# Expert output products: three fp16 products for all eight experts, instead of fp32 for two of the eight

## The reference

```
x = x + xattn(ctx, layernorm(x), Wq)       # q = x Wq, k = v = ctx Wq; causal softmax
xf = layernorm(x)
gates = softmax(xf @ gate_W); the two highest, normalised -> cw
out = xf
for e in range(8):
    h = relu(xf @ W1[e] + b1[e])           # 128 -> 256
    out = out + cw[:, e:e+1] * (h @ W2[e] + b2[e])   # 256 -> 128
x = x + out
```

## Time and profile before

| | |
|---|---|
| median of 3 runs | 142.91 us (142.78 to 143.04) |
| the profiled execution's own time | 143.2 us |
| its span, first to last instruction | 141.4 us |
| mean granted TensorE clock | 0.976 |
| PE matmul busy | 125.1 us, 88% |
| DVE busy | 104.9 us, 74% |
| ACT busy | 96.2 us, 68% |
| POOL busy | 47.3 us, 33% |

### The profile page before, as it was taken

How to read it: one execution, slowest core, us unless ns; L and a number is a source line. 1 busy time by engine, 2 the same in 40 slices (tenths; PEclk the granted TensorE clock), 3 DMA queues, 4 the chain that set the end, 5 groups by cost and what they waited for, 6 DMA issues and landing times. The chain is left out here.

```text
span 141.4 us, 3259 instructions
## 1 busy us (share of the span) xinstructions
PE 125.1 (88%) x1165; PEld 92.9 (66%) x1165; DVE 104.9 (74%) x413; ACT 96.2 (68%) x191; POOL 47.3 (33%) x53
## 2 busy tenths in 40 slices
PE   6987079789999699999998799999996999699992
PEld 2774055658786457887875468697864677467781
DVE  1529999998559799476586995885497994978573
ACT  3346354976959486796959476769685848689940
POOL 6380342703033750330127532130336603333500
PEclk9999956999999999999999999999999999999999
DMA  3999900000000000200000001000000002000002
GB/s 107 293 270 270 270 4 5 0 0 2 0 5 0 0 7 0 74 0 5 0 0 0 0 5 53 28 0 0 0 5 2 2 5 74 0 2 5 0 0 74
DMA packets 9872, 5.54 MB, mean 39 GB/s; under 512 B 472, under 2 KB 9856, under 8 KB 9856
## 3 DMA queue, kind: packets, MB, share of 16 engines
q1 hardware_dynamic: 9712, 5.27, 12.9%
q10 hardware_dynamic: 144, 0.07, 0.2%
HBM read 4.28 MB, written 1.05 MB: 38 GB/s over the span
## 5 line engine op out<-in xcount | busy, mean ns | idle before, releaser
L623 POOL TENSOR_TENSOR h_lo<-h,h_hi 128x512 f16<-128x512 f32 x24 | 27.9, 1162 | 67.7 <-ACT h L517 67.7
L517 ACT ACTIVATE h<-psH,b1T 128x512 f32<-128x512 f32 x64 | 43.5, 686 | 3.1 <-PE psH L347 1.8
L790 DVE SCALAR_TENSOR_TENSOR acc<-psY,weight_y,acc 128x128 f32<-128x128 f32 x125 | 35.1, 342 | 5.8 <-PE psY L368 5.3
L516 ACT ACTIVATE h_hi<-psH,b1T 128x512 f16<-128x512 f32 x48 | 33.0, 687 | 9.1 <-PE psH L347 9.0
L774 DVE TENSOR_TENSOR h_lo<-h,h_hi 128x512 f16<-128x512 f32 x24 | 17.3, 721 | 15.2 <-ACT h L517 15.2
L347 PE MATMUL psH<-x_lo,w_hi 128*128 128x512 f16 x62 | 23.8, 384 | 0.4
L343 PE MATMUL psH<-x_hi,w_hi 128*128 128x512 f16 x62 | 23.8, 384 | 0.0
L344 PE MATMUL psH<-x_hi,w_lo 128*128 128x512 f16 x62 | 23.8, 383 | 0.0
L368 PE MATMUL psY<-w_hi,h_hi 128*128 128x128 f16 x192 | 22.7, 219 | 0.0
L368 PE MATMUL psY<-w_lo,h_hi 128*128 128x128 f16 x192 | 22.7, 219 | 0.0
L368 PEld LDWEIGHTS psY<-w_hi,h_hi 128*128 128x128 f16 x192 | 15.4, 98 | 3.3
(11 more groups left out here) (169 smaller groups left out, 184.3 us busy)
## 6 DMA issues: line engine op xcount, KB each, us to landing
w_sb<-in_L_ffn_W_dram SPq DMA_DIRECT2D x8, 256.0 KB, 5.1
x_sb<-in_x_dram SPq DMA_DIRECT2D x1, 768.0 KB, 6.9
ctx_sb<-in_ctx_dram SPq DMA_DIRECT2D x1, 768.0 KB, 6.5
out_dram<-acc SPq DMA_DIRECT2D x3, 256.0 KB, 2.3
x_sb<-in_x_dram SPq DMA_DIRECT2D x1, 256.0 KB, 3.5
ctx_sb<-in_ctx_dram SPq DMA_DIRECT2D x1, 256.0 KB, 3.9
out_dram<-acc SPq DMA_DIRECT2D x2, 128.0 KB, 1.8
wq_sb<-in_L_xattn_Wq_dram ACTq DMA_DIRECT2D x1, 64.0 KB, 2.6
```

Of the source, the lines that this page charges most:

```text
L516: nc.scalar.activation(h_hi[:, C * (e % 2) + c, :], psH[c][:, :], ACT.Relu, bias=bias, scale=scale)
L517: nc.scalar.activation(h[:, C * (e % 2) + c, :], psH[c][:, :], ACT.Relu, bias=bias, scale=scale).then_inc(h_ready, 1)
L623: nc.gpsimd.tensor_tensor(h_lo[:, i, :], h[:, i, :], h_hi[:, i, :], ALU.subtract).then_inc(hlo0_ready, 1)
L790: last = nc.vector.scalar_tensor_tensor(out=o, in0=y, scalar=weight_y[:, t, e:e + 1], in1=o, op0=ALU.mult, op1=ALU.add)
```

## The change

Both sets become empty, so every expert of every group is split. Expert 0 changes in all four groups, expert 3 in groups 0 to 2, and expert 7 in group 3: eight expert-groups of 32.

```
--- before
+++ after
@@ -45,8 +45,8 @@
     SCALE = float(D) ** -0.5
     MASKED = 1e30
     SX, SW, SH = 16.0, 64.0, 16.0
-    FULL = (0, 3)
-    FULL_LAST = (0, 7)
+    FULL = ()
+    FULL_LAST = ()
     HB = 2 * C
     Y_FREE = 2
     WARM_UP = 9
```

## The result

The changed kernel takes 154.1 us (median of 4 runs, 152.44 to 155.15), the kernel before 142.97 us beside it (4 runs). The ratio is 1.0729 [1.0633, 1.0825]; it is taken from the executions in the fast state and so leaves out the one of 155.15 us, which was in the slow one. Slower, as forecast. The median of 154.1 us lies 0.4 us beyond the upper end of the range, that of the other three (153.97 us) 0.3 us, and the ratio times the kernel before (1.0729 x 142.97 = 153.4 us) just inside it: the result is at the edge. The profiled execution took 153.97 us, with a span of 152.2 us.

The account below looks back on a forecast made before the run. In-order ACT and DVE queues, with DVE's subtraction waiting for both halves of new h, decide, not busy PE. 1.1 + 3 x 0.95 + 2 x 1.0 + 1.3 + 1.0 = 8.25 us gives 151.2 us, range 148.5 to 153.7.

Parts of the forecast that it names:

- The direction: Whole kernel: the change makes it slower, given a chance of 0.93.
- rival A: Whole kernel: PE decides, late ACT and DVE work fits in gaps, 3.5 us faster, 139.4 us; chance 0.06.
- Prologue: Before group 0's key product: expert 0's relu ends later, delaying DVE's gate step and then ctxT; +1.1 us.
- rival C: New prologue: all of the forecast plus a clock fall during PE's idle time, +2.8 us, 154.0 us; chance 0.09.
- Boundaries: Groups 0 to 1, 1 to 2: DVE's subtraction delays gate step, ctxT and key product; +1.0 us each.
- Rival B: Boundaries and prologue: gate delay is absorbed before the key product and costs nothing; +2.1 us, 145.0 us; chance 0.09.
- Expert 3: Groups 0 to 2: ACT's extra reads delay expert 4's relu, DVE's subtraction, residual and xf transposes; +0.95 us each.
- Last boundary: Into the last group: late gate chain, with L754 held by POOL's subtraction, delays weight_cat; +1.3 us.
- The end: Last group: DVE's subtraction waits for expert 7's relu and stands ahead of the last sums; +1.0 us.
- The sum: All terms from prologue to end added: 8.25 us, giving 151.2 us; forecast's chance 0.72.

Follow-up runs that it names:

- e4: Changed kernel with DVE's subtraction for the next group's expert 0 moved behind the gate step, prologue included; 148.51 us.
- e2: Kernel before with expert 0 alone split, in all four groups; 149.4 us.
- e6: Changed kernel with five matmuls on zeros filling PE's gap ahead of each group's xf transposes; 151.26 us.
- e7: Kernel before with ACT also writing an unread h_hi for the fp32 experts, products and DVE and POOL work unchanged; 145.46 us.
- e5: e4 with the last group's expert 7 back in fp32 and DVE's sums of experts 2 and 3 ahead of subtractions for experts 3 and 4; 143.78 us.
- e8: Changed kernel with POOL's last-group subtraction for expert 2 waiting until DVE has written weight_cat; 153.17 us.
- e3: Kernel before with only expert 7 of the last group split; 144.6 us.
- e10: Kernel before with only POOL's last-group subtraction for expert 2 made to wait until weight_cat is written; 142.83 us.
- e1: Kernel before with expert 3 alone split, in groups 0 to 2; 147.79 us.
- e9: e5 with POOL's last-group wait of e8 added; 143.59 us.

## Why the prediction was right, and where it failed

- **The direction, and rival A.** Right. Each split product saves PE its 0.44 us and the kernel is 11 us slower. PE is the busiest engine and the change relieves it; the end is set by what PE waits for.
- **Prologue, +1.1.** Measured +1.10; e4 takes it away by DVE's order alone. PE's wait for ctxT is 1.05 us there, not the 1.9 us of rival C's working; its products before it run at the low clock until 27.1 us, before until 23.9.
- **Boundaries, +1.0 each from the queues.** Right as the cause: +1.05 in e2 and e6, where the clock holds; nothing with ACT's reads alone (e7); nothing with the gate step first (e4). Rival B is out by the same rows.
- **Expert 3, +0.95 each.** The mechanism is right: of what was added, ACT's two reads alone do it (e7), by way of DVE's subtraction for expert 4 (e5). The size was a little high: 0.82 to 0.87 us (1.04 in group 0). The working added 0.95 us to the start of probsT and took the rest as before. But probsT no longer waits for PE, and the next relu follows 0.47 us behind its start, not 0.59 us. The two relus together end 0.81 us later.
- **Last boundary, +1.3.** Measured +1.29, with the stall on L754 as forecast, and e8 takes the stall away.
- **The end, +1.0.** Measured +1.01, and +0.99 alone (e3). ACT's reads make 0.45 us of it (e7).
- **The sum.** With the clock held the queue terms give 151.26 us (e6), where 151.2 was forecast. By the stretches they are 10.80 less 2.67 for the falls, 8.13 us, where 8.25 was added up. A part of this closeness is luck: expert 3 was put too high in two groups and too low in the third, and each boundary 0.05 us too low.
- **The step that failed** is the price of the clock: the sum has no term for it, and rival C, "all of the forecast, and a low clock on top", got a chance of 0.09. It is what happened. It was looked for in the prologue, priced by the one long stretch at the start (5.7 us, +2.8 us), and set against one gap of 1.43 us that "left the clock alone". The profile after shows two falls, in groups 0 and 1, each behind the gap before the xf transposes. By e6 they cost 1.31 and 1.36 us: 2.67 of the 2.75 us by which the boundaries exceed their 2.0. That rival C's 154.0 us is next to the measured 154.1 us is luck, since its 2.8 us were worked out for another place. The low stretch at the start got longer too (to 27.1 us, before to 23.9), without a price: e4 has it as long, and its prologue is the 10.97 us of before. The prediction said that the gap before the xf transposes should grow, and did not ask what the clock would do behind it. And one execution in which the clock held after 1.43 us was taken as a rule. In further runs of the kernel before only 16 of 22 had the mean clock of the profiled one; the profiles of e3, e8 and e10 show a fall at that place, behind gaps of 2.05, 1.47 and 2.09 us.
- **Open.** What decides, between two gaps of equal length, which one is followed by a fall; why expert 3's term is 1.04 us in group 0 and 0.82 in e1 (in the changed kernel DVE's `weight_cat` operation L765 takes 1.03 us there beside POOL's subtraction, and 0.19 us in e1, but no run takes that away); the 1.75 us of the last store in e2, and the like in e9; the 1.3 us outside the span in e1.

## What to carry to other kernels

Before adding an instruction, walk the queue that it stands in: what is behind it, who waits for that, and which stage is without slack; here the work of eight cheaper products cost 8 us by standing ahead of a gate step, a residual and the last sums, and changed orders brought seven of them to 0.7 us over the kernel before (1.5 us by the stretches). If a step lengthens an idle gap of TensorE in the middle of a dense stream, price a fall of the clock behind it (here 1.31 to 1.36 us each), and read several executions before saying that the clock holds. Where VectorE and GpSimd both work on SBUF, look for the short operations of a critical chain that last as long as the other engine's: one wait on the side that has time bought 0.75 us of that chain.

## What the runs showed of the hardware

- The granted clock fell to 0.50 behind gaps of 1.45 to 1.47 us before the xf transposes, in a stream that was otherwise dense: in 6 of 12 such gaps in the profiles of the changed kernel, e1, e4 and e8. Behind those of 1.11 to 1.31 us there (the kernel before, e2, e3, e5, e7, e9, e10) it never fell. Length alone does not decide: the wait of 1.83 us before weight_cat's transposes was followed by no fall in the changed kernel, nor in e2, e4 and e6, and one of 1.87 us at e1's first key product neither, while 1.47 us in e8, 2.05 us in e3 and 2.09 us in e10 at that product were.
- The times of one kernel spread in steps with the mean clock: the changed kernel took 152.44 us at a mean clock of 0.951 and 153.97 and 154.23 us at 0.944, the kernel before 142.78 us at 0.976 and 143.69 us at 0.961 to 0.964 (medians of 16 and six runs).
- A 128x32 operation of DVE took 1.13 us instead of 0.19 us while POOL's 1.16 us subtraction ran, and 0.19 us again once POOL's was moved (e8).
